# A fused convolution block: the last channel group finished bank by bank, with half snapshots and x added by VectorE

## The chip, the cores and the metric

The kernel runs on one core of a Trainium2 chip. The metric is the device time of one execution in microseconds (us). Its engines are TensorE (PE, matmuls), VectorE (DVE), ScalarE (ACT), GpSimd (POOL, used here mostly to issue DMAs) and SyncE (SP, which only issues DMAs). TensorE writes into PSUM banks; the other tiles named here lie in SBUF. DMAs move data between SBUF and HBM, whoever issues them, on the same 16 DMA engines.

## The reference

x has the shape (16, 256, 56, 56). The reference adds to x the product of a convolution and a map:

```python
xn = (x - mean) * lax.rsqrt(var + EPS)          # of the group-normed x, over batch and pixels
xn = xn * bn_gamma[None, :, None, None] + bn_beta[None, :, None, None]
t = jnp.where(xn >= 0.0, 1.0, 0.0)
t = jnp.where(xn <= 0.0, -1.0, t).astype(xn.dtype)
xc = jnp.clip(xn, -1.0, 1.0)
c_sum = jnp.sum(xc * t, axis=1, keepdims=True)
c_cnt = jnp.sum(jnp.abs(t), axis=1, keepdims=True)
y = _conv_nchw(t, conv_w, STRIDE, PAD) + conv_b[None, :, None, None]      # 3x3, 256 to 256 channels
b_sum = _conv_nchw(c_sum, ones_k, STRIDE, PAD) + beta_conv_b[0]
b_cnt = _conv_nchw(c_cnt, ones_k, STRIDE, PAD) + beta_conv_b[0]
return y * (b_sum / b_cnt)
...
x = x + _L0_conv_ref(_gn(x), ...)
```

## The kernel before

**Tiling.** An image n (0 to 15) is worked on in four groups g. A group is one half of the 256 output channels (g % 2, 128 partitions) times one half of the rows (g // 2, 28 rows, 1568 pixels for each partition). The 28 rows are 7 quads of four rows; `quads(t)` is the view [partition, quad, row of the quad, column]. The 3x3 convolution is done with a transform along the rows: for each quad six planes of transformed input (`V`) are multiplied with six planes of transformed weights (`U`), and each product plane has one row per quad, 7 x 56 = 392 elements.

**Products.** `products` (line 558) issues 24 matmuls of 128x128 weights by 385 or 392 columns: 12 (`TERMS`) into each of two PSUM banks, `acc[:, g % 2, bank]`. A group gets three such calls: `first`, `second` and `third`. They accumulate into the same two banks. After `first`, and again after `second`, ScalarE copies both banks to `sn` (`snapshot`, line 435, one ACTIVATE of 784 elements), and TensorE waits for the copy (`snap1`, `snap2`) before it goes on, since the snapshot must not contain the next planes. For image n TensorE's order (`image`, line 595) is first(g), third(g - 1), second(g) for g = 0 to 3, so that a snapshot is normally covered by another group's block. After image 15 only `third(15, 3)` is left (line 628), directly behind `second(15, 3)`.

**From products to output.** VectorE does for each group:
- `mid` (line 844): `ds` from the two snapshots (784 elements, line 849), then the rows 1 and 2 of each quad into `y` (lines 854 and 856).
- `ends` (line 860), after `third`: rows 0 and 3 of each quad from the two banks of `acc` and from `ds` (line 865, twice 392 elements).
- `finish` (line 870): y = (y + conv bias) * map, 1568 elements (line 877).
Then POOL's queue adds x by an accumulating load of x into y (line 335) and stores y (line 330), in the order: load of group s, store of group s - 1. A `mid` waits for the store of the group of the image before that used the same part of y (`y_out[g]`).

**The last group.** For (15, 3) there is no accumulating load. `finish` is done in two parts (`LAST_PARTS`, by contiguous pixels, 784 each), and `add_last` (line 880) adds x by VectorE from `xb`, which still holds image 15. SP stores each part as it comes (line 282): 128 rows of 3136 bytes. VectorE's order at the end (lines 955 to 971) is mid(15,0), ends(15,0), finish(14,3), mid(15,1), ends(15,1), finish(15,0), mid(15,2), finish(15,1), ends(15,2), finish(15,2), mid(15,3), ends(15,3), and then finish and add for each part. ScalarE's last instructions (lines 518 to 521) are the snapshots alone.

Other names: `crow`, `sum_rows`, `bm` and `map_rows` carry the map (its rows of 56 floats, 224 bytes, are written to HBM at line 246 and its sums are read back at line 217); `sum_rows` is written at line 213 in pieces of 128 bytes.

Of the kernel before, what the change touches and what calls it, by code (L numbers as in the profile page):

```python
# [8 lines left out]
ALU = mybir.AluOpType  # L9
# [29 lines left out]

LAST_PARTS = ((0, N // 2), (N // 2, N))  # L40


def conv_preact(nc, x, w_t, gamma, beta, conv_b, beta_b, consts, sum_rows, map_rows, out):
# [6 lines left out]
    with ExitStack() as ctx:  # L50
# [63 lines left out]
        y_out = [sem(f"y_out{g}") for g in range(G4)]  # L114
        last_out = [sem(f"last_out{k}") for k in range(2)]
        x_added = [sem(f"x_added{g}") for g in range(G4)]
# [68 lines left out]
        def _(sp):  # L185
# [93 lines left out]

            for k, (lo, hi) in enumerate(LAST_PARTS):  # L280
                sp.wait_ge(last_added, k + 1)
                sp.dma_start(out_v[NI - 1, 1, 1][:, 4 * lo:4 * hi], y[:, 3, 4 * lo:4 * hi]).then_inc(last_out[k], 16)
            for g in range(G4):

                sp.wait_ge(y_out[g], 16 * (NI - (g == 3)))
            for k in range(2):
                sp.wait_ge(last_out[k], 16)
# [3 lines left out]
        def _(pool):  # L291
# [39 lines left out]

            for s in range(G4 * NI - 1):
                n, g = divmod(s, G4)
                pool.wait_ge(scaled, s + 1)
                pool.dma_start(y[:, g], x_v[n, g % 2, g // 2], accum_op=ALU.add).then_inc(x_added[g], 16)  # L335
                if s:
                    store(s - 1)
            store(G4 * NI - 2)


        @block.scalar
        def _(act):
# [174 lines left out]
            channel_sums(last)  # L517
            for g in range(1, G4):
                snapshot(last, g - 1, 1)
                snapshot(last, g, 0)  # L520
            snapshot(NI - 1, 3, 1)


        @block.tensor
        def _(pe):
# [31 lines left out]

            def products(n, a, g, planes, done, by_channels=False, banks=(0, 1)):

                h, co = g // 2, g % 2  # L560
                for part in range(CT if by_channels else 1):
                    if by_channels:
                        pe.wait_ge(v_first, part + 1)
                    for bank in banks:
                        k = planes[bank]
                        for i, (ci, digits, dx) in enumerate(TERMS):
                            if by_channels and ci != part:
                                continue
                            lo, hi = max(0, 1 - dx), W - max(0, dx - 1)
                            last = nc.tensor.matmul(  # L570
                                by_row(acc[:, g % 2, bank, 0:N])[:, :, lo:hi],
                                U[:, ci, digits, k, dx, co * P:(co + 1) * P],
                                by_row(V[:, a, ci, VPLANE[k], h])[:, :, lo + dx - 1:hi + dx - 1],
                                start=(planes is FIRST and i == 0),
                                stop=(planes is THIRD and i == len(TERMS) - 1), skip_group_check=True)
                if 1 in banks:
                    last.then_inc(done, 1)

            def first(n, a, g, by_channels=False, banks=(0, 1)):

                if 0 in banks:
                    at_least(pe, y03_done, 4 * n + g - 1)
                products(n, a, g, FIRST, first_done, by_channels, banks)

            def second(n, a, g):

                pe.wait_ge(snap1, 4 * n + g + 1)
                products(n, a, g, SECOND, second_done)

# [4 lines left out]

            def image(n, a):
                for g in range(G4):
                    if g % 2 == 0:
                        pe.wait_ge(v_ready, 4 * n + 2 + g)
                    first(n, a, g)
                    if g == 0:  # L600
                        quarter_sums(n)
                    third(n - 1, 1 - a, 3) if g == 0 else third(n, a, g - 1)
                    second(n, a, g)

# [19 lines left out]
            with pe.Fori(0, (NI - 2) // 2) as i:  # L624
                image(2 * i + 1, 1)
                image(2 * i + 2, 0)
            image(NI - 1, 1)
            third(NI - 1, 1, 3)


        @block.vector
        def _(dve):
# [236 lines left out]

            def finish(n, g, part=None):  # L870

                s, b, h = 4 * n + g, g % 2, g // 2
                lo, hi = (4 * at for at in part or (0, N))
# [3 lines left out]
                nc.vector.scalar_tensor_tensor(out=y[:, g, lo:hi], in0=y[:, g, lo:hi], scalar=vec[:, 2, b:b + 1],  # L877
                                               in1=bmap[:, h, lo:hi], op0=ALU.add, op1=ALU.mult).then_inc(scaled, 1)

            def add_last(k):  # L880

                lo, hi = (4 * at for at in LAST_PARTS[k])
                dve.wait_ge(scaled, G4 * NI + k)
                nc.vector.tensor_tensor(y[:, 3, lo:hi], y[:, 3, lo:hi], own_rows(3)[:, lo:hi], ALU.add)\  # L884
                  .then_inc(last_added, 1)
# [125 lines left out]
```

## Time and profile before

| | us |
|---|---|
| median of 3 runs | 937.71 |
| lowest, highest | 937.62, 938.79 |
| profiled execution | 937.77 |
| its span, first to last instruction | 936.0 |
| TensorE busy | 782.9 |
| VectorE busy | 790.4 |
| ScalarE busy | 581.3 |
| POOL busy | 140.8 |

The span is the profiler's time from the first to the last instruction; 1.77 us of the profiled execution lie outside it. Times in rows are from the start of the span. The profile names an instruction by its line of the kernel before, its engine and its operands, `out<-in`. Until 175 us the statistics and the weights are prepared; then the images run at an even pace, and the last image's groups are done from some 880 us on.

### The profile page before, as it was taken

The page shows a single profiled execution, that of the slowest core. Times are in us where ns is not written, and L with a number is a line of the kernel's source. Part 1 is how long each engine was busy: PE and PEld are TensorE (multiplying, and loading weights), DVE is VectorE, ACT ScalarE, POOL GpSimd, SP SyncE. Part 2 cuts the span into 40 slices and gives each one's busy share as a digit, 9 for nine tenths or more (in the row PEclk, how much of TensorE's full clock was granted, in tenths as well). Part 3 has the DMA queues.
Part 4 walks back from the last instruction along what each step waited for, and adds up shares of the span by engine and source line. Part 5 has one row for each costly group of instructions (what it writes and reads, how often), then busy time and mean ns, then how long its engine had stood idle before and what let it go on. Part 6 is the DMA issues. An engine that isn't in the chain of part 4 may idle for free. (4 is left out here: it accounts for less than half of the span.)

```text
span 936.0 us, 12745 instructions
## 1 busy us (share of the span) xinstructions
PE 782.9 (84%) x4686; PEld 464.9 (50%) x4686; DVE 790.4 (84%) x1244; ACT 581.3 (62%) x469; POOL 140.8 (15%) x160
## 2 busy tenths in 40 slices
PE   2100003999999999999999999999999999999996
PEld 2100002555555555555555555555555555555553
DVE  4999998989888888888797979787878797879755
ACT  2043105968777777777777777776868686868310
POOL 0089300001111111101111111111111111101011
PEclk9755555999999999999999999999999999999998
DMA  9999972468888887888797969696969696958589
GB/s 360 429 408 377 411 323 70 142 182 259 252 249 231 243 238 220 265 213 275 192 296 174 314 161 318 163 310 165 308 171 297 174 297 185 293 157 215 131 214 268
DMA packets 43478, 232.79 MB, mean 249 GB/s; under 512 B 10560, under 2 KB 10688, under 8 KB 39360
## 3 DMA queue, kind: packets, MB, share of 16 engines
q0 software_dynamic: 18144, 101.16, 41.8%
q1 hardware_dynamic: 24544, 131.25, 38.7%
q10 hardware_dynamic: 768, 0.12, 0.1%
q8 instruction: 9, 0.15, 0.1%
q14 instruction: 13, 0.11, 0.0%
HBM read 180.73 MB, written 51.79 MB: 248 GB/s over the span
## 5 line engine op out<-in xcount | busy, mean ns | idle before, releaser
L570 PE MATMUL acc<-V,U 128*128 128x385 f16 (+1 forms) x4608 | 769.4, 331 | 11.8 <-DVE V L790 10.1
L570 PEld LDWEIGHTS acc<-V,U 128*128 128x128 f16 x4608 | 450.9, 98 | 325.8 <-issue 12.7
L442 ACT ACTIVATE sn<-acc,inv_s 128x784 f32<-128x784 f32 x128 | 116.9, 913 | 207.1 <-PE acc L570 201.2
L335 POOL DMA_DIRECT2D y<-x x63 | 53.9, 856 | 728.7 <-DVE y L877 715.2
L877 DVE SCALAR_TENSOR_TENSOR y<-y,vec,bmap 128x1568 f32<-128x1568 f32 (+1 forms) x65 | 117.7, 1810 | 0.2
L420 ACT ACTIVATE r<-xb,ab 128x1568 f32<-128x1568 f32 x64 | 106.6, 1690 | 6.0 <-ACT u L395 4.0
L395 ACT ACTIVATE u<-xb,ab 128x1624 f16<-128x1624 f32 x63 | 109.0, 1732 | 0.2
L405 ACT ACTIVATE T<-u 128x1680 f16<-128x1680 f16 x60 | 95.6, 1594 | 2.0 <-DVE D L784 2.0
L408 ACT ACTIVATE T<-T 128x1568 f16<-128x1568 f16 x58 | 87.6, 1510 | 1.8
L543 PE MATMUL csum<-mv,cst 128*128 128x32 f32 x2 | 0.6, 396 | 94.9 <-DVE mv L654 94.9
L784 DVE TENSOR_TENSOR D<-T 128x1568 f16<-128x1568 f16 x63 | 61.4, 974 | 15.1 <-ACT T L408 14.3
L849 DVE SCALAR_TENSOR_TENSOR ds<-sn 128x784 f32<-128x784 f32 x64 | 62.0, 968 | 5.9 <-ACT sn L442 5.9
L662 DVE BATCH_NORM_STATS2 st<-y 128x6 f32<-128x448 f32 x112 | 60.2, 600 | 6.6 <-DMA y<-x 6.5
L819 DVE SCALAR_TENSOR_TENSOR ssum<-r 128x1568 f32<-128x1568 f32 x32 | 57.3, 1791 | 3.5 <-ACT r L426 2.0
L826 DVE TRANSPOSE_TENSOR_REDUCE quarter<-ssum 128x49 f32<-128x1568 f32 x32 | 57.8, 1805 | 0.1
L662 DVE BATCH_NORM_STATS2 st<-xb 128x6 f32<-128x448 f32 x98 | 52.6, 598 | 6.1 <-DMA xb<-x 6.1
L330 POOL DMA_DIRECT2D out<-y x63 | 51.7, 821 | 9.9 <-DMA y<-x 9.3
L777 DVE TENSOR_SCALAR T<-T 128x784 f16<-128x784 f16 x64 | 22.5, 351 | 32.8 <-ACT T L405 32.6
L426 ACT ACTIVATE r<-r 128x1568 f32<-128x1568 f32 x32 | 48.4, 1511 | 1.0
L865 DVE SCALAR_TENSOR_TENSOR y<-acc,inv_s,ds 128x392 f32<-128x392 f32 x64 | 39.7, 620 | 9.8 <-PE acc L570 9.8
L543 PEld LDWEIGHTS csum<-mv,cst 128*128 128x128 f32 x2 | 0.5, 313 | 94.9 <-issue 94.9
L854 DVE SCALAR_TENSOR_TENSOR y<-sn,ds 128x392 f32<-128x392 f32 x64 | 36.3, 568 | 9.3 <-DMA out<-y 2.7
(99 smaller groups left out, 396.2 us busy)
## 6 DMA issues: line engine op xcount, KB each, us to landing
xb<-x SPq DMA_DIRECT2D x64, 812.0 KB, 6.4
y<-x POOLq DMA_DIRECT2D x63, 784.0 KB, 7.7
out<-y POOLq DMA_DIRECT2D x63, 784.0 KB, 9.4
y<-x SPq DMA_DIRECT2D x16, 1568.0 KB, 8.3
bmap<-map_rows SPq DMA_DIRECT2D x32, 784.0 KB, 6.1
xb<-x SPq DMA_DIRECT2D x14, 1568.0 KB, 8.7
V<-w_t SPq DMA_DIRECT2D x2, 1152.0 KB, 14.6
out<-y SPq DMA_DIRECT2D x2, 392.0 KB, 2.8
```

The lines of the kernel that those rows point to most:

```text
L395: nc.scalar.activation(u[:, g % 2, 1:1 + XR], by_row(xb[:, c, g // 2]), ACT.Sign, scale=ab[:, a, 0, c:c + 1], bias=ab[:, a, 1, c:c + 1])\
L405: nc.scalar.activation(T[:, 30:60], u[:, g % 2, h:h + HR + 2], ACT.Relu, scale=2.0).then_inc(t_ready, 1)
L408: nc.scalar.activation(T8[:, :], T[:, 30:30 + HR], ACT.Copy, scale=4.0, bias=-3.0)\
L420: nc.scalar.activation(r[:, c, 0:HPX], own_rows(g), ACT.Abs, scale=ab[:, a, 0, c:c + 1], bias=ab[:, a, 1, c:c + 1]).then_inc(abs_done, 1)
L442: nc.scalar.activation(sn[:, b, half], acc[:, b, :, 0:N], ACT.Copy, scale=inv_s[:, b:b + 1])\
L570: last = nc.tensor.matmul(by_row(acc[:, g % 2, bank, 0:N])[:, :, lo:hi], U[:, ci, digits, k, dx, co * P:(co + 1) * P], by_row(V[:, a, ci, ...
L662: ins = nc.vector.bn_stats(st[:, a, c, j], stat_buffer(a, c)[:, j * PIECE:(j + 1) * PIECE])
L784: nc.vector.tensor_tensor(d[:, 0], T[:, 32:32 + HR], T8[:, :], ALU.subtract).then_inc(cq_done, 1)
L819: nc.vector.scalar_tensor_tensor(out=ssum[:, :], in0=r[:, 0, 0:HPX], scalar=1.0, in1=r[:, 1, 0:HPX], op0=ALU.min, op1=ALU.subtract).then_i ...
L826: nc.vector.tensor_reduce(quarter[:, h, :], ssum[:, :].rearrange("p (b i) -> p b i", i=SQ), AX.X, ALU.add, apply_transpose=True).then_inc( ...
L849: nc.vector.scalar_tensor_tensor(out=ds[:, :, :], in0=sn[:, b, 0], scalar=2.0, in1=sn[:, b, 1], op0=ALU.mult, op1=ALU.subtract).then_inc(d ...
L877: nc.vector.scalar_tensor_tensor(out=y[:, g, lo:hi], in0=y[:, g, lo:hi], scalar=vec[:, 2, b:b + 1], in1=bmap[:, h, lo:hi], op0=ALU.add, op ...
```

## The change

Four things are changed, all for the last groups of image 15.

TensorE: `first(15, 3)` is issued for bank 0, then `third(15, 2)`, then `first(15, 3)` for bank 1. In each of first, second and third of (15, 3) a semaphore is raised after bank 0 as well as at the end, and the waits for snapshots are by bank.

ScalarE: each of the two snapshots of (15, 3) is taken as two halves, one a bank.

VectorE: `last_mid` forms `ds` bank by bank; `last_end(k)` forms row 0 (k = 0) or row 3 (k = 1) of each quad when that bank's third products are done; `last_finish(k)` then finishes and adds x for rows 0 to 2, and afterwards for row 3 (`LAST_ROWS`). `add_x(2)` adds x for the whole of (15, 2).

Queues: POOL no longer loads x for (15, 2) nor stores it; SP stores (15, 2) after `add_x(2)`, and then the two parts of (15, 3): per partition 7 pieces of 3 rows (672 bytes), and 7 pieces of one row (224 bytes).

```diff
-LAST_PARTS = ((0, N // 2), (N // 2, N))
+LAST_ROWS = ((0, 3), (3, 4))
...
-            for k, (lo, hi) in enumerate(LAST_PARTS):
-                sp.wait_ge(last_added, k + 1)
-                sp.dma_start(out_v[NI - 1, 1, 1][:, 4 * lo:4 * hi], y[:, 3, 4 * lo:4 * hi]).then_inc(last_out[k], 16)
+            sp.wait_ge(last_added, 1)
+            sp.dma_start(out_v[NI - 1, 0, 1], y[:, 2]).then_inc(last_out[2], 16)
+            for k, (lo, hi) in enumerate(LAST_ROWS):
+                sp.wait_ge(last_added, k + 2)
+                sp.dma_start(quads(out_v[NI - 1, 1, 1])[:, :, lo:hi].rearrange("p q i w -> p q (i w)"),
+                             quads(y[:, 3])[:, :, lo:hi].rearrange("p q i w -> p q (i w)")).then_inc(last_out[k], 16)
...
-            for s in range(G4 * NI - 1):
+            for s in range(G4 * NI - 2):
...
-            store(G4 * NI - 2)
+            store(G4 * NI - 3)
...
-            for g in range(1, G4):
+            for g in range(1, G4 - 1):
                 snapshot(last, g - 1, 1)
                 snapshot(last, g, 0)
-            snapshot(NI - 1, 3, 1)
+            snapshot(last, 2, 1)
+            act.wait_ge(mid_done, G4 * NI - 2)
+            for half, done, part_done, snap, part_snap in ((0, first_done, first_half, snap1, snap1_half),
+                                                           (1, second_done, second_half, snap2, snap2_half)):
+                for bank in range(2):
+                    if bank:
+                        act.wait_ge(done, G4 * NI)
+                    else:
+                        act.wait_ge(part_done, 1)
+                    nc.scalar.activation(sn[:, 1, half, bank], acc[:, 1, bank, 0:N], ACT.Copy, scale=inv_s[:, 1:2])\
+                      .then_inc(snap if bank else part_snap, 1)
...
+                        if half is not None and bank == 0:
+                            last.then_inc(half, 1)
+                            if planes is SECOND:
+                                pe.wait_ge(snap1, G4 * NI)
+                            if planes is THIRD:
+                                pe.wait_ge(snap2, G4 * NI)
                 if 1 in banks:
                     last.then_inc(done, 1)
...
-                    first(n, a, g)
+                    last = final and g == 3
+                    if last:
+                        first(n, a, g, banks=(0,), half=first_half)
+                    else:
+                        first(n, a, g)
                     if g == 0:
                         quarter_sums(n)
                     third(n - 1, 1 - a, 3) if g == 0 else third(n, a, g - 1)
-                    second(n, a, g)
+                    if last:
+                        first(n, a, g, banks=(1,))
+                    second(n, a, g, second_half if last else None)
...
-            image(NI - 1, 1)
-            third(NI - 1, 1, 3)
+            image(NI - 1, 1, final=True)
+            pe.wait_ge(snap2_half, 1)
+            products(NI - 1, 1, 3, THIRD, third_done, half=third_half)
...
+            def add_x(g):
+
+                dve.wait_ge(scaled, G4 * NI - 3 + g)
+                nc.vector.tensor_tensor(y[:, g], y[:, g], own_rows(g), ALU.add).then_inc(last_added, 1)
+
+            def last_mid():
+
+                last = G4 * NI
+                for bank in range(2):
+                    if bank:
+                        dve.wait_ge(snap2, last)
+                    else:
+                        dve.wait_ge(snap2_half, 1)
+                        dve.wait_ge(y03_done, last - 1)
+                    ins = nc.vector.scalar_tensor_tensor(out=ds[:, bank], in0=sn[:, 1, 0, bank], scalar=2.0,
+                                                         in1=sn[:, 1, 1, bank], op0=ALU.mult, op1=ALU.subtract)
+                ins.then_inc(ds_done, 1)
+                dve.wait_ge(y_out[3], 16 * (NI - 1))
+                dve.wait_ge(ds_done, last)
+                yq = quads(y[:, 3])
+                nc.vector.scalar_tensor_tensor(out=yq[:, :, 1], in0=by_row(sn[:, 1, 1, 1]), scalar=2.0,
+                                               in1=by_row(ds[:, 0]), op0=ALU.mult, op1=ALU.add)
+                nc.vector.scalar_tensor_tensor(out=yq[:, :, 2], in0=by_row(ds[:, 1]), scalar=4.0,
+                                               in1=by_row(sn[:, 1, 1, 0]), op0=ALU.mult, op1=ALU.add)\
+                  .then_inc(mid_done, 1)
+                dve.wait_ge(mid_done, last)
+
+            def last_end(k):
+
+                if k:
+                    dve.wait_ge(third_done, G4 * NI)
+                else:
+                    dve.wait_ge(third_half, 1)
+                nc.vector.scalar_tensor_tensor(
+                    out=quads(y[:, 3])[:, :, 3 * k], in0=by_row(acc[:, 1, k, 0:N]), scalar=(inv_s, inv_8)[k][:, 1:2],
+                    in1=by_row(ds[:, 1 - k]), op0=ALU.mult, op1=ALU.add).then_inc(y03_done, 1)
+                dve.wait_ge(y03_done, G4 * NI + k)
+
+            def last_finish(k):
+
+                lo, hi = LAST_ROWS[k]
+                part = lambda t: quads(t)[:, :, lo:hi].rearrange("p q i w -> p q (i w)")
+                dve.wait_ge(bmap_in[1], 16 * NI)
+                nc.vector.scalar_tensor_tensor(out=part(y[:, 3]), in0=part(y[:, 3]), scalar=vec[:, 2, 1:2],
+                                               in1=part(bmap[:, 1]), op0=ALU.add, op1=ALU.mult).then_inc(scaled, 1)
                 dve.wait_ge(scaled, G4 * NI + k)
-                nc.vector.tensor_tensor(y[:, 3, lo:hi], y[:, 3, lo:hi], own_rows(3)[:, lo:hi], ALU.add)\
+                nc.vector.tensor_tensor(part(y[:, 3]), part(y[:, 3]), part(own_rows(3)), ALU.add)\
                   .then_inc(last_added, 1)
...
-            mid(NI - 1, 3)
-            ends(NI - 1, 3)
+            add_x(2)
+            last_mid()
             for k in range(2):
-                finish(NI - 1, 3, LAST_PARTS[k])
-                add_last(k)
+                last_end(k)
+                last_finish(k)
```

## Rows read from the trace of the kernel before

**Rows 1.** The page's head and part 1: busy us, share of span, instructions.

```profile
span 936.0 us, 12745 instructions
PE 782.9 (84%) x4686; PEld 464.9 (50%) x4686; DVE 790.4 (84%) x1244; ACT 581.3 (62%) x469; POOL 140.8 (15%) x160
```

**Rows 2.** Chain that ended last, its last pieces: start, us, what.

```profile
931.08 1.04 DVE y L877
...
932.14 0.98 DVE y L884
```

**Rows 3.** Timeline from 910 us: start, us, engine, line, out<-in, count [idle before].

```profile
910.52 0.86 POOL L330 DMA_DIRECT2D out<-y  x1
...
913.74 1.85 DVE L877 SCALAR_TENSOR_TENSOR y<-y,vec,bmap 128x1568 f32<-128x1568 f32 x1
914.73 0.91 ACT L442 ACTIVATE sn<-acc,inv_s 128x784 f32<-128x784 f32 x1 [3.07 <-PE acc L570]
...
918.72 0.63 DVE L865 SCALAR_TENSOR_TENSOR y<-acc,inv_s,ds 128x392 f32<-128x392 f32 x1 [3.13 <-PE acc L570]
...
922.70 0.91 ACT L442 ACTIVATE sn<-acc,inv_s 128x784 f32<-128x784 f32 x1 [7.06 <-PE acc L570]
923.42 0.56 POOL L330 DMA_DIRECT2D out<-y  x1 [0.46 <-DMA y<-x]
923.65 0.97 DVE L849 SCALAR_TENSOR_TENSOR ds<-sn 128x784 f32<-128x784 f32 x1 [1.83 <-ACT sn L442]
...
923.67 4.16 PE L570 MATMUL acc<-V,U 128*128 128x392 f16 x24 [1.01 <-ACT sn L442]
924.73 0.57 DVE L854 SCALAR_TENSOR_TENSOR y<-sn,ds 128x392 f32<-128x392 f32 x1
925.22 0.56 DVE L856 SCALAR_TENSOR_TENSOR y<-ds,sn 128x392 f32<-128x392 f32 x1
927.87 0.63 DVE L865 SCALAR_TENSOR_TENSOR y<-acc,inv_s,ds 128x392 f32<-128x392 f32 x1 [2.10 <-PE acc L570]
928.41 0.62 DVE L865 SCALAR_TENSOR_TENSOR y<-acc,inv,ds 128x392 f32<-128x392 f32 x1
929.12 1.03 DVE L877 SCALAR_TENSOR_TENSOR y<-y,vec,bmap 128x784 f32<-128x784 f32 x1
...
930.19 0.97 DVE L884 TENSOR_TENSOR y<-y,xb 128x784 f32<-128x784 f32 x1
...
931.19 2.29 SPq L282 DMA_DIRECT2D out<-y  x2
```

**Rows 4.** DMA view of 933.9 to 935.1: busy tenths in 30 ns slices; SP's queue: packets, MB, share.

```profile
DMA  0009829927597759775977595779777997753000
...
q1 hardware_dynamic: 146, 0.40, 84.9%
```

**Rows 5.** Groups of instructions, shapes apart: ACT's pass over 1568 elements, busy us, mean ns.

```profile
L420 ACT ACTIVATE r<-xb,ab 128x1568 f32<-128x1568 f32 x64 | 106.6, 1690 | 6.0 <-ACT u L395 4.0 <-DVE ssum L819 0.5
```

**Rows 6.** Line 330, the one store issued between 910 and 911 us.

```profile
DMA to landing us min/median/max: 8.3/8.3/8.3
```

**Rows 7.** Busy time by stretch, last column GB/s: with an accumulating load, then without.

```profile
925.00:927.00 2.00, 2.00 (x14) 1.17 (x12) 0.78 (x2) 0.00 (x0) 0.00 (x0) 1.00 0.87 166
...
931.00:933.00 2.00, 0.00 (x0) 0.00 (x0) 1.97 (x3) 0.00 (x0) 0.00 (x0) 0.50 0.99 403
```

**Rows 8.** Waits of SP's queue over the span: us in total, times, longest.

```profile
SPq L217 <- DMA sum_rows<-cs: 79.5, 16, 6.2
```

**Rows 9.** DMA view, 887.0 to 887.5 (`crow` read), then 889.9 to 890.5 (`bm` written).

```profile
DMA  0000000000000014634644589699877696532210
...
q1 hardware_dynamic: 175, 0.04, 37.9%
...
DMA  0000000000000000004554535321000000000000
...
q1 hardware_dynamic: 70, 0.01, 10.3%
```

More of the change, by code:

```diff
@@ L114, in conv_preact @@
         y_out = [sem(f"y_out{g}") for g in range(G4)]
-        last_out = [sem(f"last_out{k}") for k in range(2)]
+        last_out = [sem(f"last_out{k}") for k in range(3)]
+        first_half, second_half, third_half = sem("first_half"), sem("second_half"), sem("third_half")
+        snap1_half, snap2_half = sem("snap1_half"), sem("snap2_half")
         x_added = [sem(f"x_added{g}") for g in range(G4)]
@@ L278, in _ @@
             image(NI - 1)
-            for k, (lo, hi) in enumerate(LAST_PARTS):
-                sp.wait_ge(last_added, k + 1)
-                sp.dma_start(out_v[NI - 1, 1, 1][:, 4 * lo:4 * hi], y[:, 3, 4 * lo:4 * hi]).then_inc(last_out[k], 16)
+            sp.wait_ge(last_added, 1)
[4 more added lines that the diff above has]
+                             quads(y[:, 3])[:, :, lo:hi].rearrange("p q i w -> p q (i w)")).then_inc(last_out[k], 16)
             for g in range(G4):
-                sp.wait_ge(y_out[g], 16 * (NI - (g == 3)))
-            for k in range(2):
+                sp.wait_ge(y_out[g], 16 * (NI - (g > 1)))
+            for k in range(3):
                 sp.wait_ge(last_out[k], 16)
@@ L556, in quarter_sums, with products @@
                                  cst[:, C_FOLD:C_FOLD + SQ], start=True, stop=True).then_inc(cs_done, 1)
-            def products(n, a, g, planes, done, by_channels=False, banks=(0, 1)):
+            def products(n, a, g, planes, done, by_channels=False, banks=(0, 1), half=None):
                 h, co = g // 2, g % 2
@@ L575, in products, with first, second @@
                                 stop=(planes is THIRD and i == len(TERMS) - 1), skip_group_check=True)
+                        if half is not None and bank == 0:
[4 more added lines that the diff above has]
+                                pe.wait_ge(snap2, G4 * NI)
                 if 1 in banks:
                     last.then_inc(done, 1)
-            def first(n, a, g, by_channels=False, banks=(0, 1)):
+            def first(n, a, g, by_channels=False, banks=(0, 1), half=None):
                 if 0 in banks:
                     at_least(pe, y03_done, 4 * n + g - 1)
[L583 to L588, printed above, removed]
+                products(n, a, g, FIRST, first_done, by_channels, banks, half)
+            def second(n, a, g, half=None):
+                if half is None:
+                    pe.wait_ge(snap1, 4 * n + g + 1)
+                else:
+                    pe.wait_ge(snap1_half, 1)
+                products(n, a, g, SECOND, second_done, half=half)
             def third(n, a, g):
@@ L593, in third, with image @@
                 products(n, a, g, THIRD, third_done)
-            def image(n, a):
+            def image(n, a, final=False):
                 for g in range(G4):
@@ L868, in ends, with finish @@
                 ins.then_inc(y03_done, 1)
-            def finish(n, g, part=None):
+            def finish(n, g):
                 s, b, h = 4 * n + g, g % 2, g // 2
-                lo, hi = (4 * at for at in part or (0, N))
                 dve.wait_ge(mid_done, s + 1)
@@ L876, in finish @@
                 dve.wait_ge(bmap_in[h], 16 * n + 16)
[L877 to L882, printed above, removed]
+                nc.vector.scalar_tensor_tensor(out=y[:, g], in0=y[:, g], scalar=vec[:, 2, b:b + 1],
+                                               in1=bmap[:, h], op0=ALU.add, op1=ALU.mult).then_inc(scaled, 1)
@@ new lines, in last_end @@
+            def last_end(k):
+                if k:
+                    dve.wait_ge(third_done, G4 * NI)
+                else:
+                    dve.wait_ge(third_half, 1)
[9 more added lines that the diff above has]
+                                               in1=part(bmap[:, 1]), op0=ALU.add, op1=ALU.mult).then_inc(scaled, 1)
```

## The prediction

> **What bounds the kernel now.** I read three views in this order: the page's first part, the chain that ended last, and the timeline of the last 25 us. The page shows TensorE busy for 84% of the span [rows 1]; the reader should take from it only that the middle is a full pipeline which this change doesn't touch. Everything edited belongs to image 15, groups 2 and 3, so the question is what ends after about 910 us. The chain ends on VectorE: the second half of `finish` and `add_last` [rows 2]. The timeline [rows 3] shows what stands before it. TensorE's blocks of 24 matmuls follow each other at 3.99 us: `first(15,3)` ends 0.04 us before ACT's snapshot at 914.73, `third(15,2)` 0.04 before VectorE's `ends` at 918.72, `second(15,3)` 0.04 before the snapshot at 922.70. (The 0.04 is the step from TensorE's end, 923.67 + 4.16 = 927.83, to `ends` at 927.87.) So `second(15,3)` ends at 922.66, TensorE then stands 1.01 us for the full snapshot, runs `third(15,3)` to 927.83, and only there VectorE's serial tail begins: two `ends` instructions, finish, add, finish, add, to 932.14 + 0.98 = 933.12 [rows 2, 3]. The last store is then issued at about 933.14, its packets run from 933.99 to 935.00 [rows 4], and the span ends at 936.00, 1.00 after the last packet. The profiled execution took 937.77 us, 1.77 outside the span; the median of the runs shown is 937.71, so the sum below, made against 937.77, can be 0.06 high.
>
> **TensorE's new order.** `first(15,3)` is split by banks and `third(15,2)` put between. Nothing is added to the work, so the total stays at four blocks of 3.99 from 910.70: first bank 0 to 912.69, `third(15,2)` to 916.68, first bank 1 to 918.68, second bank 0 to 920.67, bank 1 to 922.66. `third(15,2)` starts 2 us earlier and needs the snapshot taken at 910.70 + 0.04, done 0.91 later (911.65): 1.04 us of slack. The half snapshots: ACT takes 0.913 for 784 elements [rows 3] and 1.690 for 1568 [rows 5], 0.99 ns an element, so 0.53 for 392. Each is done 1.4 us before the bank that waits for it (bank 0 of second: its snapshot is over at 919.3 at the latest; third bank 0: 921.3 against 922.66; third bank 1: 923.3 against 924.66). The 1.01 us stall goes, and third runs 922.66 to 924.66 and to 926.65. The cost is three more boundaries with a semaphore ahead of second's end. A block has 8 x 392 + 16 x 385 = 9296 columns, 3.87 us at the full level of 2.4 GHz, and takes 3.99, so a boundary costs from 0 to 0.12 us (not below 0: no matmul is dropped). I take 0.03 each, 0.10 in all, up to 0.35.
>
> **VectorE ahead of the tail.** With `third(15,2)` done at 916.68, `ends(15,2)` starts at 916.72, after `finish(15,1)` is over at 915.59 [rows 3]; it and `finish(15,2)` (1.85, by the same row) end at 919.8. `add_x(2)` is new: an add of 1568 elements; the 784-element add took 0.97 [rows 3] and another 784 elements cost 0.81 (1.85 - 1.03, finish whole less finish half), so 1.78, to 921.6. Behind it on VectorE waits ds of bank 0, ready at 921.3: 0.57, over at 922.2, before bank 1's snapshot at 923.3. So it is hidden by 1.1 us of idle time; without that cover it would cost its 1.78. `last_mid` also waits for the store of group (14,3), issued at 910.52 [rows 3] and landed 8.3 us later [rows 6], some four microseconds early.
>
> **VectorE's tail.** Gaps by rows of before: 0.04 after ACT; 0.11 from ds to the instruction that needs it (924.62 to 924.73); 0.49 from start to start of the two mid instructions; 0.09 behind a mid or an `ends` whose result is waited for; 0.04 from finish to add; an unrelated next one starts 0.09 before the end of an add (930.19 + 0.97 against 931.08) [rows 2, 3]. With the 0.10: second ends at 922.76, ACT 922.80 to 923.33, ds bank 1 (0.57) 923.37 to 923.94, mid 924.05 and 924.54 to 925.10. Then `ends` bank 0 925.19 to 925.81 (third bank 0 is done by 924.8, so VectorE, not TensorE, decides from here), finish of three rows in four, 1176 elements, 1.03 + 0.40 = 1.43, 925.90 to 927.33; its add 0.97 + 0.40 = 1.37, 927.37 to 928.74; `ends` bank 1 928.65 to 929.27; finish of 392 elements 0.63, 929.36 to 929.99; add 0.57, 930.03 to 930.60. Against 933.12 that is 2.52 us earlier: 1.0 from the stall, the rest because mid and bank 0's end and finish run under third.
>
> **The queues.** The accumulating load and the store of (15,2) leave POOL, and SP stores (15,2) itself at 921.6. SP's following waits (for the two last parts) stand behind an issue of 0.34 us only. What is in flight from 921.7: the end of the accumulate of (15,1), the stores of (15,0) and (15,1) (the latter issued at 923.42 [rows 3], behind that accumulate as now) and SP's: 3 x 128 x 1568 x 4 B, 2.4 MB. Plain stores moved 403 GB/s, a stretch with an accumulate 166 [rows 7]; so 6.0 us and about 1 more for what remains of the accumulate: empty at 928.7 to 929. The first last part is issued at 928.76 with its first packet 0.85 later (933.14 to 933.99), at 929.6: clear by 0.6 us. It must be, for a small store behind this traffic landed badly: SP waited 79.5 / 16 = 5.0 us for each 98-row store of `sum_rows` [rows 8].
>
> **The scattered last stores.** They were 128 packets of 3136 B each. Now they follow rows: 7 pieces for each of 128 partitions, 896 packets of 672 B and 896 of 224 B, 56 each for an engine and one for the semaphore. Nearest rows: the 3136 B packets took 0.849 x 16 x 1.2 / 146 = 0.112 each with the semaphores' (about 0.125 without) [rows 4]; the 224 B reads of `crow` 0.379 x 16 x 0.5 / 175 = 0.017 of busy time; their busy stretch is some 25 slices of 12.5 ns for 13 packets an engine, 0.024 in elapsed time (the `bm` store of 56 rows shows 70 packets, 14 over, so I read one completion each on 14 engines; `crow` has 168 rows, 12 an engine and the completion); the 224 B writes of `bm` 0.103 x 16 x 0.6 / 70 = 0.014 of busy time, and elapsed ten slices of 15 ns for 5, 0.030 [rows 9]. By the line between 0.017 and 0.125, 672 B takes 0.034: 1.9 us, to 931.5. The last part, issued at 930.62, has its first packet at 931.5 too; 57 packets take 1.0 (busy time of the reads), 1.4 (their elapsed time) or 1.7 (elapsed of the writes). I take 1.4, since five packets are mostly ramp, and keep both ends. Last packet at 932.9, span's end 1.00 later, at 933.9: 2.1 us earlier. This gives back 0.4 of the 2.5. 937.77 - 2.1 = 935.7.
>
> The rule of the Trainium skill that speaks against this part is in "DMA: Bandwidth & Descriptors", Specifications: transfers under 512 B fall below line rate because the engine does a read-modify-write. The `bm` writes of 224 B don't show it in busy time, 0.014 against 0.017 for reads [rows 9]. By the rule, taken as twice the 1.0, the last part would take 1.9 to 2.0 and the time be 936.2 to 936.3; the same direction is rival 1, priced from rows.
>
> **The rivals.** (1) Short rows cost more when written in bulk. For it: the elapsed 0.030 of the only 224 B writes, 0.013 over the 0.017; against it: their busy time of 0.014. With 0.030 for the last part and 0.034 + 0.013 for the 672 B rows: 929.6 + 2.7 + 1.7 = 934.0, end 935.0, time 936.8. (2) The queues aren't empty at 929.6, since the stores move at 300 GB/s beside the accumulate instead of 403: they clear about 1 us late, 936.7. For it: stretches with an accumulate are slow; against: 0.6 us of margin and none issued after 915.88. (3) All the small terms fall well: boundaries free (0.1), last part at busy pace (0.4): 935.2. (4) Slower: the same last stores, at a pace like that of the `sum_rows` rows. The time is 929.6 + 114 t + 1.0 + 1.77 for a pace of t an engine and packet: equal to before at t = 0.047, slower by 0.2% from t = 0.064, and 941.5 at 0.08. For it: `sum_rows` with 7 packets an engine took 5 us; against: that one stood behind POOL's traffic, and the `crow` rows kept 0.024. (5) The change does not do what it says: a half's snapshot comes late or `add_x` holds VectorE, so that ds of bank 1 starts no earlier than 924.4; then half the gain stays, 936.8.
>
> **How the numbers follow.** Forecast 935.7 (its own range 935.2 to 936.2) 0.52; rival 3 0.13; rival 1 0.18; rival 2 0.07; rival 5 0.04; rival 4 0.06. The range leaves out rival 4 and the outer ends: 934.9 to 937.4. A measurement of this kernel tells about 0.2% from no change, 1.88 us, so faster by more means below 935.83: 0.6 of the forecast's 0.52 and rival 3's 0.13, with a little of the others, 0.47. Slower 0.06, and within 0.2% 0.47.
>
> **What would show it.** Right: no idle time of TensorE between `second(15,3)` and third, and its last matmul at 926.7 to 926.9; VectorE without a gap over 0.15 us from ds bank 1 (923.3 to 923.6) to its last add, which ends at 930.4 to 930.9; `add_x(2)` over before 922; the packets of SP's last two stores from 929.6 to 932.5 to 933.6. Wrong: last add early and packets past 934 (rival 1 or 4); other queues' packets after 929.6 (rival 2); a wait for ACT or a late start of ds bank 1 (rival 5).

## The result and the profile after

| | before | after |
|---|---|---|
| median of 13 runs each, us | 938.22 | 935.95 |
| lowest, us | 937.28 | 934.99 |
| profiled execution, us | 937.77 | 936.13 |
| its span, us | 935.97 | 934.32 |

The ratio is 0.9970, with a 95% interval of 0.9959 to 0.9980: faster by 0.3%, and the interval ends just at 0.2%. The page gives a span to a tenth of a microsecond; the traces keep nanoseconds, and those are used here: 935.97 and 934.32. The two differ by only 1.65 us, less than the medians (2.27). The reason can be seen as soon as both timelines are laid side by side: in the profiled execution of after, image 15 is 0.80 us late before anything that was changed is reached. So all that follows is counted from one mark which no kernel here moves, the start of ScalarE's snapshot after `first(15,2)`: at 902.77 before and 903.57 after. From there to the end of the span it is 33.20 us before and 30.75 after, 2.45 less; two later profiles of the same changed kernel gave 30.75 again. (The expectations below were written with the rounded spans, 33.23 and 30.73, and a tail of 3.11 and 2.88 where the traces have 3.13 and 2.85.) The mark in the timeline of before:

```profile
902.77 0.91 ACT L442 ACTIVATE sn<-acc,inv_s 128x784 f32<-128x784 f32 x1 [3.07 <-PE acc L570]
```

The timeline of after (start, us, engine, line, operation, out<-in, [idle before]) at the instructions that answer to [rows 3]. L585 is the matmul, L535 the half snapshots, L896 the first `ends` instruction of (15,2), L913 `add_x`, L924 to L956 the last group:

```profile
902.70 24.75 PE L585 MATMUL acc<-V,U 128*128 128x385 f16 x148
...
903.57 0.91 ACT L447 ACTIVATE sn<-acc,inv_s 128x784 f32<-128x784 f32 x1 [3.07 <-PE acc L585]
...
917.52 0.63 DVE L896 SCALAR_TENSOR_TENSOR y<-acc,inv_s,ds 128x392 f32<-128x392 f32 x1 [1.15 <-PE acc L585]
...
920.65 1.79 DVE L913 TENSOR_TENSOR y<-y,xb 128x1568 f32<-128x1568 f32 x1
...
923.50 0.59 ACT L535 ACTIVATE sn<-acc,inv_s 128x392 f32<-128x392 f32 x1 [1.41 <-PE acc L585]
...
924.12 0.57 DVE L924 SCALAR_TENSOR_TENSOR ds<-sn 128x392 f32<-128x392 f32 x1 [1.19 <-ACT sn L535]
924.79 0.57 DVE L930 SCALAR_TENSOR_TENSOR y<-sn,ds 128x392 f32<-128x392 f32 x1
925.27 0.56 DVE L932 SCALAR_TENSOR_TENSOR y<-ds,sn 128x392 f32<-128x392 f32 x1
925.87 0.63 DVE L943 SCALAR_TENSOR_TENSOR y<-acc,inv_s,ds 128x392 f32<-128x392 f32 x1
926.53 1.44 DVE L953 SCALAR_TENSOR_TENSOR y<-y,vec,bmap 128x1176 f32<-128x1176 f32 x1
928.01 1.38 DVE L956 TENSOR_TENSOR y<-y,xb 128x1176 f32<-128x1176 f32 x1
929.31 0.62 DVE L943 SCALAR_TENSOR_TENSOR y<-acc,inv,ds 128x392 f32<-128x392 f32 x1
929.42 2.18 SPq L286 DMA_DIRECT2D out<-y  x2
929.96 0.63 DVE L953 SCALAR_TENSOR_TENSOR y<-y,vec,bmap 128x392 f32<-128x392 f32 x1
930.62 0.57 DVE L956 TENSOR_TENSOR y<-y,xb 128x392 f32<-128x392 f32 x1
```

Three things are to be seen. TensorE is one piece to 927.45; the idle 1.01 us of [rows 3] is gone. From the mark its last matmul ends 1.18 us earlier: the 1.01, and 0.17 because `third(15,3)` takes the 3.99 us of the other blocks and not the 4.16 that it took after the wait [rows 3]. From 924.12 VectorE has one instruction behind the other, none with an idle time of note, to 930.62 + 0.57 = 931.19. And from there to the span's end it is 3.13 us, where it was 2.85 (933.12 to 935.97). So VectorE's last add ends 2.73 us earlier from the mark (27.63 for 30.35), and what follows it is 0.28 longer.

The DMA view of after, 926 to 935 in slices of 0.225 us, against [rows 4] and [rows 7]:

```profile
DMA  9999999999983000000499999999999600000000
GB/s 446 418 418 418 418 418 446 418 446 418 418 335 140 0 0 0 0 0 0 155 329 317 323 320 317 317 248 286 278 271 268 142 1 0 0 0 0 0 0 0
```

This view counts a packet where it starts. The last packet of the groups before starts at 928.92 and ends at 929.16; the engines then stand idle until 930.36, when the first of the two last stores begins. The 672-byte pieces move at about 320 GB/s, the 224-byte ones at about 270, and the last packet ends at 933.23.

### The profile page after: what moved, and what is told of

It reads as the page before. It is cut to its first block, busy times and chain, and to the rows that moved or that the text cites. A ratio compares the mean times of both kernels' runs of the same rounds, so it can differ in the third digit from the quotient of the medians.

```text
span 934.3 us, 12748 instructions
## 1 busy us (share of the span) xinstructions
PE 781.9 (84%) x4686; PEld 464.5 (50%) x4686; DVE 792.2 (85%) x1246; ACT 582.1 (62%) x471; POOL 139.7 (15%) x158
## 4 chain that ended last, share of the span: by engine, by line
PE 77%; DVE 17%; DMA 3%; issue 2%; ACT 1%; SPq 0%; DVEq 0%; ACTq 0%
PE acc L585 77%; DVE st L693 11%; DMA xb<-x 2%; DVE st L704 1%; DMA sum_rows<-cs 1%; DVE y L907 1%; DVE D L815 0%; ACT r L425 0%; DVE y L896 0%; DVE ds L880 0%; DVE V L825 0%; DVE y L953 0%; DVE D L813 0%; DVE V L826 0%; DVE quarter L857 0%
## 5 line engine op out<-in xcount | busy, mean ns | idle before, releaser
L585 PE MATMUL acc<-V,U 128*128 128x385 f16 (+1 forms) x4608 | 769.6, 330 | 10.8 <-DVE V L821 10.1
L585 PEld LDWEIGHTS acc<-V,U 128*128 128x128 f16 x4608 | 451.3, 98 | 324.6 <-issue 13.1
L907 DVE SCALAR_TENSOR_TENSOR y<-y,vec,bmap 128x1568 f32<-128x1568 f32 x63 | 115.6, 1835 | 0.1
L808 DVE TENSOR_SCALAR T<-T 128x784 f16<-128x784 f16 x64 | 22.5, 351 | 32.8 <-ACT T L410 32.6
L896 DVE SCALAR_TENSOR_TENSOR y<-acc,inv_s,ds 128x392 f32<-128x392 f32 x63 | 39.1, 620 | 5.8 <-PE acc L585 5.8
```

Source lines behind the costliest of these rows:

```text
L585: last = nc.tensor.matmul(by_row(acc[:, g % 2, bank, 0:N])[:, :, lo:hi], U[:, ci, digits, k, dx, co * P:(co + 1) * P], by_row(V[:, a, ci, ...
L907: nc.vector.scalar_tensor_tensor(out=y[:, g], in0=y[:, g], scalar=vec[:, 2, b:b + 1], in1=bmap[:, h], op0=ALU.add, op1=ALU.mult).then_inc( ...
```

## The experiments

All nine edits were judged from the mark, since the median of a few runs can't tell parts of a microsecond of this kernel. "Tail" is the time from the end of VectorE's last add to the end of the span. Ratios are to the kernel before on the same chip.

**Only TensorE's and ScalarE's part**

```diff
# of the changed kernel, back as before (SP's last two stores too):
-            add_x(2)
-            last_mid()
-            for k in range(2):
-                last_end(k)
-                last_finish(k)
+            mid(NI - 1, 3)
+            ends(NI - 1, 3)
+            for k in range(2):
+                finish(NI - 1, 3, LAST_PARTS[k])
+                add_last(k)
...
+            for s in range(G4 * NI - 1):       # POOL loads and stores (15,2) again
```

> Only TensorE's and ScalarE's part of the change: first(15,3) by banks with third(15,2) between, half snapshots. VectorE, POOL and SP as before. All cases are counted from one mark that the change doesn't touch, the start of ScalarE's snapshot after first(15,2), to the end of the span: 33.23 us before, 30.73 after. Theory (the stall of 1.01 us stood on the path, and all VectorE work behind third moves with it): TensorE has no idle time between second and third of group 3, ends starts 1.2 us earlier from the mark, VectorE's tail keeps its 5.25 us, mark to end 32.0. Rival (VectorE's own work in front of ends, or POOL's store of group 2, is next in line at once): ends starts 0.4 us earlier at most, mark to end 32.8.

Measured: mark (904.50) to end 32.65; ratio 0.9997 (0.9982 to 1.0012). The timeline:

```profile
925.05 0.98 DVE L877 SCALAR_TENSOR_TENSOR ds<-sn 128x784 f32<-128x784 f32 x1 [3.50 <-ACT sn L532]
...
928.42 0.63 DVE L893 SCALAR_TENSOR_TENSOR y<-acc,inv_s,ds 128x392 f32<-128x392 f32 x1 [1.24 <-PE acc L582]
...
931.04 0.55 POOL L332 DMA_DIRECT2D out<-y  x1 [5.45 <-DMA y<-x]
...
931.74 2.29 SPq L284 DMA_DIRECT2D out<-y  x2
932.69 0.97 DVE L912 TENSOR_TENSOR y<-y,xb 128x784 f32<-128x784 f32 x1
```

The theory's VectorE part holds: `ends` starts 23.92 after the mark instead of 25.10, and the last add ends at 933.66, 29.17 after it, 1.19 earlier than before. But the end of the span is only 0.56 earlier, nearer to the rival's 32.8 than to the theory's 32.0: the tail is 3.48 us. The rival was right in naming POOL's store of group 2, though not in a late `ends`: that store is issued at 931.04 and SP's last stores from 931.74, so that both are in the queues together for longer than before (there 929.70 and 931.19). The gain of the stall is real and half of it is lost; that the DMA queues take it is shown by the run after the next.

**Only group (15,2)**

```diff
# of the kernel before:
-            for s in range(G4 * NI - 1):
+            for s in range(G4 * NI - 2):
...
+            sp.wait_ge(x2_added, 1)
+            sp.dma_start(out_v[NI - 1, 0, 1], y[:, 2]).then_inc(last_out[2], 16)
...
+            add_x(2)
             mid(NI - 1, 3)
```

> Only the part on group (15,2): VectorE adds its x and SP stores it, POOL's accumulating load and store of it are gone; group 3 as before. Theory: nothing, mark to end 33.1 to 33.3 (from 33.23), since the add of 1.79 us lies in VectorE's idle time ahead of the last ds and the last store of before was not behind POOL's packets. Rival (POOL's traffic held up the last stores): the first of the two last stores lands in 2.3 us instead of 3.2 and the span ends 0.5 us earlier, 32.7. Rival (the added instruction delays the last mid): 33.6 or more.

Measured: mark (903.46) to end 33.26, VectorE's last add 30.35 after the mark, as before; ratio 0.9997 (0.9988 to 1.0007). By itself this part is worth nothing (the end is even 0.06 later): the theory.

**Banks and group 2, with the old tail of group 3**

```diff
# the two edits above together; VectorE's end is
+            add_x(2)
             mid(NI - 1, 3)
             ends(NI - 1, 3)
```

> The banks-only kernel with group (15,2) moved as in the change (VectorE adds x, SP stores), while group 3 keeps the old tail: one ds of 784 elements, both ends, then finish and add by contiguous halves. Theory (the two parts need each other: banks give 1.2 us only if POOL's accumulate and store are out of the way): VectorE's last add ends 29.15 us after the mark, as with banks only, and the span 2.9 later, at 32.05, where banks only had 32.6 and group 2 only 33.24. What is left to the change's 30.72 is then the bank-wise tail of group 3. Rival (the late last stores of the banks-only run had another cause): tail of 3.4, 32.6.

Measured: mark (903.69) to end 32.08, last add 29.17, tail 2.91; ratio 0.9997 (0.9983 to 1.0010).

```profile
930.94 2.29 SPq L287 DMA_DIRECT2D out<-y  x2
931.89 0.97 DVE L920 TENSOR_TENSOR y<-y,xb 128x784 f32<-128x784 f32 x1
```

The last add is where it was with the banks alone, and the tail is that of the run with group 2 alone (2.91), so it was POOL's traffic that had stretched it to 3.48. (This interval can't see the 1.12 us, 0.12%; the timeline can.)

**The change without its group (15,2)**

```diff
# of the changed kernel:
-            for s in range(G4 * NI - 2):
+            for s in range(G4 * NI - 1):
...
-            add_x(2)
             last_mid()
```

> The changed kernel, but group (15,2) goes through POOL's queue again (accumulating load, then store), without VectorE's add of it. Theory (from the banks-only run, where VectorE's last add ended 29.16 us after the mark and the last stores then stood behind POOL's store of group 2): POOL's store is still issued about 26.5 us after the mark, when the accumulating load has landed, the first of SP's last stores meets it, and the span ends 32.0 to 32.8 after the mark instead of 30.73, with VectorE's last add still at 27.6. Rival (the DMA engines have room for both): 30.7 to 31.0. Rival (the short pieces take turns with POOL's packets of 6272 bytes and crawl): 34 or more.

Measured: mark (903.81) to end 33.31; ratio 1.0000 (0.9988 to 1.0013). The direction was foreseen, the size (32.0 to 32.8) was not: the whole gain is gone, with VectorE as early as in the changed kernel. Its timeline, and its DMA queues from 930 us to the end (queue: packets, MB, share of the engines; then SP's two stores: KB, us from issue to landing):

```profile
929.67 2.19 SPq L284 DMA_DIRECT2D out<-y  x2
930.21 0.55 POOL L333 DMA_DIRECT2D out<-y  x1 [5.17 <-DMA y<-x]
930.22 0.63 DVE L951 SCALAR_TENSOR_TENSOR y<-y,vec,bmap 128x392 f32<-128x392 f32 x1
930.88 0.57 DVE L954 TENSOR_TENSOR y<-y,xb 128x392 f32<-128x392 f32 x1
```

```profile
q0 software_dynamic: 229, 1.24, 43.5%
q1 hardware_dynamic: 1824, 0.80, 39.8%
...
out<-y SPq DMA_DIRECT2D x1, 588.0 KB, 6.1
out<-y SPq DMA_DIRECT2D x1, 196.0 KB, 5.2
```

The last add ends at 931.44, 27.63 after the mark, and 5.68 us follow it. POOL's queue still moves 1.24 MB after 930.0; SP's two stores land 6.1 and 5.2 us after issue instead of 3.5 and 2.5. The engines are busy for 83% of these 7.1 us, and the last 1.1 us of them come behind the last packet; each of SP's packets takes as long as in the changed kernel (0.034 and 0.016 us by the trace). So this is a queue of bytes in front of the last ones, not a crawl.

**`third(15,2)` not put between the banks**

```diff
# of the changed kernel:
-                        first(n, a, g, banks=(0,), half=first_half)
+                        first(n, a, g, half=first_half)
...
-                    if last:
-                        first(n, a, g, banks=(1,))
```

> The changed kernel, but first(15,3) runs whole before third(15,2); half snapshots and bank-wise second and third stay. Theory (the order matters only by letting VectorE finish group 2 earlier): TensorE has no stall either way, third(15,2) ends 2 us later, the x add of group 2 ends about 1.9 us later, the ds of bank 1 starts 0.8 us late, mark to end 31.5 instead of 30.73. Rival (it serves to cover the snapshots): a stall of 0.5 us on TensorE comes back. Rival (the order is worth nothing): 30.7.

Measured: mark (904.58) to end 31.46, close to the theory; ratio 0.9984 (0.9973 to 0.9995).

```profile
900.72 27.74 PE L585 MATMUL acc<-V,U 128*128 128x385 f16 x166
...
923.66 1.79 DVE L911 TENSOR_TENSOR y<-y,xb 128x1568 f32<-128x1568 f32 x1
...
925.37 1.03 DVE L922 SCALAR_TENSOR_TENSOR ds<-sn 128x392 f32<-128x392 f32 x2
```

TensorE is one piece without the interleaving too (to 928.46, 23.88 after the mark, as in the changed kernel), so the half snapshots, with their waits by bank, remove the stall without it. What the new order brings is 0.71 us, and on VectorE: the x add of group 2 ends 2 us earlier, so both halves of ds no longer wait behind it.

**The last stores contiguous** (from x, so that group (15,3) of the output is x alone)

```diff
-                sp.dma_start(quads(out_v[NI - 1, 1, 1])[:, :, lo:hi].rearrange("p q i w -> p q (i w)"),
-                             quads(y[:, 3])[:, :, lo:hi].rearrange("p q i w -> p q (i w)")).then_inc(last_out[k], 16)
+                sp.dma_start(out_v[NI - 1, 1, 1][:, N * lo:N * hi], own_rows(3)[:, N * lo:N * hi]).then_inc(last_out[k], 16)
```

> The changed kernel with its last two stores made contiguous: 4704 and 1568 bytes for each partition, taken from x instead of y (so the output of group (15,3) is x alone; the waits and all computation stay). Theory (the pieces of 672 and 224 bytes cost 0.4 us): last add's end to the span's end 2.7 us instead of 3.11, mark to end 30.3. Rival (short pieces cost nothing in bulk): 3.1 and 30.7. Rival (they cost double and more, a write below 512 bytes being read first): under 2.5 and under 30.1.

Measured: mark (904.05) to end 30.09, tail 2.47; ratio 0.9968 (0.9952 to 0.9984). Against the 3.13 of the changed kernel, the short pieces cost 0.66 us, more than the theory's 0.4. By the expectation's numbers this would be the double price of a short write; the next experiment shows it isn't.

**All rows of group (15,3) in pieces of 224 bytes**

```diff
+                for i in range(lo, hi):
+                    sp.dma_start(quads(out_v[NI - 1, 1, 1])[:, :, i], quads(y[:, 3])[:, :, i]).then_inc(last_out[k], 16)
```

> The changed kernel with the first of the two last stores cut into three stores of single rows, so that all four rows go in pieces of 224 bytes (3584 instead of 1792 packets for the same bytes). It measures what a 224-byte packet costs in bulk. Theory (0.0155 us of a DMA engine for each, as the last store's packets show): 112 more packets an engine, where 56 of 672 bytes (0.031 each) are replaced by 168: 2.6 us instead of 1.7, span's end 0.9 us later, mark to end 31.6. Rival (a store under 512 bytes costs double): 168 at 0.031 or more, 5.2 us, mark to end 34 or more. Rival (SP's issue of 0.38 us for each of the four stores sets the pace): 31.5 as well, but with idle DMA engines between the stores.

Measured, in one execution: mark (903.70) to end 32.07, tail 4.44. The DMA view from 930.5 to 934.5:

```profile
DMA  7999899999888999898888989988899999999994
...
q1 hardware_dynamic: 3646, 0.80, 100.9%
```

One short packet took 1.009 x 16 x 4.0 / 3646 = 0.0177 us, in a full queue of 3646, at 201 GB/s. The reads of [rows 9] had 0.017. The end at 32.07 is far from the 34 of the double price, and the engines have no idle stretch between the stores, so SP's issue does not set the pace either. The excess of 0.47 us over the theory's 31.6 is about what 0.0177 in place of 0.0155 makes in 228 packets an engine (0.50).

In the changed kernel itself the two sizes can be read apart, 672 bytes from 930.5 to 931.5 and 224 bytes from 932.5 to 932.9:

```profile
DMA packets 479, 0.32 MB, mean 322 GB/s; under 512 B 0, under 2 KB 479, under 8 KB 479
q1 hardware_dynamic: 479, 0.32, 98.7%
...
DMA packets 483, 0.11 MB, mean 270 GB/s; under 512 B 483, under 2 KB 483, under 8 KB 483
q1 hardware_dynamic: 483, 0.11, 117.2%
```

A packet of 672 bytes takes 0.987 x 16 x 1.0 / 479 = 0.033 us, one of 224 bytes 1.172 x 16 x 0.4 / 483 = 0.0155. A share above 100% means that packets of one engine overlap: one starts every 16 x 0.4 / 483 = 0.013 us. Why the same pieces go at 270 GB/s here and at 201 when 3646 of them stand in the queue was not isolated.

**POOL takes a part of the tail** (a version made to be faster)

```diff
+            nc.gpsimd.tensor_tensor(e0, by_row(ds[:, 1]), quads(bmap[:, 1])[:, :, 0], ALU.mult)
...
+            nc.gpsimd.tensor_tensor(e0, e0, quads(own_rows(3))[:, :, 0], ALU.add)
...
+            nc.gpsimd.tensor_tensor(rows12(y[:, 3]), rows12(y[:, 3]), rows12(own_rows(3)), ALU.add)
```

> A version made to be faster. x plus bias times map of group (15,3) is formed early in an idle stretch of VectorE (1.84 us); ds of bank 0 times map plus that, for row 3, in the idle 1.2 us before ds of bank 1; the same for row 0 and the x add of rows 1 and 2 on POOL (about 0.92 and 1.84 us, from 2.35 ns an element in its 768-element instructions, beside VectorE). After third only one product with the map for each bank and one add of 784 elements are left, then one contiguous store of the whole group by SP. Theory (VectorE's serial work after the last snapshot is the bound): VectorE's last add ends 25.6 us after the mark instead of 27.6, the store needs 3.9 us from there to the span's end (2.88 for half of it, and 1.0 for the other half's packets), mark to end 29.5 instead of 30.73. Rival (POOL beside a busy VectorE is slower than alone, and its two products for row 0 and its add are then last): 30.7 or more.

Measured: mark (904.23) to end 31.42, last add 27.54 after the mark; ratio 0.9986 (0.9974 to 0.9997). The rival's time. Its timeline:

```profile
925.53 1.37 POOL L348 TENSOR_TENSOR ssum<-ds,bmap 128x392 f32<-128x392 f32 x1
925.94 1.39 DVE L955 SCALAR_TENSOR_TENSOR y<-ds,sn 128x392 f32<-128x392 f32 x1
926.98 1.22 POOL L350 TENSOR_TENSOR ssum<-ssum,xb 128x392 f32<-128x392 f32 x1
927.36 1.67 DVE L960 TENSOR_TENSOR y<-y,bmap 128x784 f32<-128x784 f32 x1
...
929.11 1.84 POOL L352 TENSOR_TENSOR y<-y,xb 128x784 f32<-128x784 f32 x1 [0.91 <-DVE y L960]
929.49 0.61 DVE L967 SCALAR_TENSOR_TENSOR y<-acc,inv,bmap 128x392 f32<-128x392 f32 x1
930.13 1.64 DVE L973 TENSOR_TENSOR y<-y,ssum 128x784 f32<-128x784 f32 x1
```

But POOL's instructions are not last, as the rival had it: they made VectorE's longer, an instruction of 0.56 took 1.39, two of 0.97 took 1.67 and 1.64. POOL's two short ones became longer too, 1.37 and 1.22 for the expected 0.92; its long add kept the expected 1.84. The two engines took turns: L955 ends 0.43 us after POOL's L348, POOL's L350 0.87 after L955, L960 0.83 after L350, and L973 0.82 after POOL's add, each a little less than the instruction needs alone (0.56, the expected 0.92, 0.97 and 0.97). L967, with one input in PSUM, kept its 0.61 beside POOL's add. The Trainium skill ("SBUF — State Buffer", Who interferes with whom) has the rule: a VectorE instruction with two SBUF inputs contends with a GpSimd instruction that reads SBUF, over a pair of ports that one of them locks, and one with at most one SBUF input (outside the modes that use both of VectorE's port pairs) does not contend. The trace agrees with both halves. The tail, with one contiguous store of the whole group, was 3.87, near the expected 3.9.

**The rows finished one after the other, without POOL** (a version made to be faster)

```diff
+                nc.vector.tensor_tensor(by_row(e[:, 1]), by_row(ds[:, 0]), bq[:, :, 3], ALU.mult).then_inc(e_step, 1)
...
+                nc.vector.tensor_tensor(by_row(e[:, 1]), by_row(e[:, 1]), xq[:, :, 3], ALU.add).then_inc(e_step, 1)
...
+                times_map_and_x(1, 3, 1)
...
+                nc.vector.tensor_tensor(yq[:, :, 3], yq[:, :, 3], by_row(e[:, 1]), ALU.add).then_inc(last_added, 1)
...
+                times_map_and_x(0, 1, 2)
```

> A version made to be faster, without POOL. x plus bias times map of group (15,3) is formed early in an idle stretch of VectorE, and ds of bank 0 times map plus that, for row 3, in the idle 1.2 us before ds of bank 1. Then rows 1 and 2 are finished and stored, then row 3 (one product and one add after third), then row 0 (three instructions), each stored by SP in pieces of 448, 224 and 224 bytes. Theory (VectorE's serial work bounds the last add; the last store should be small): last add ends 27.2 us after the mark instead of 27.6, last store's packets 28.05 to 29.1, mark to end 30.15 instead of 30.72, that is 0.06% faster than the changed kernel. Rival (more short pieces keep the DMA engines busy past VectorE's end): 30.7 or more. Rival (the added 1.84 us instruction delays group 2's mid and all behind it): last add later than 27.6.

Measured: mark (904.12) to end 30.12; ratio to before 0.9963 (0.9947 to 0.9979), where the changed kernel beside it had 0.9978 (0.9966 to 0.9990).

```profile
928.44 3.25 SPq L289 DMA_DIRECT2D out<-y  x3
928.98 0.57 DVE L970 TENSOR_TENSOR y<-y,ssum 128x392 f32<-128x392 f32 x1
929.47 0.62 DVE L971 SCALAR_TENSOR_TENSOR y<-acc,inv_s,ds 128x392 f32<-128x392 f32 x1
930.12 0.57 DVE L958 TENSOR_TENSOR y<-y,bmap 128x392 f32<-128x392 f32 x1
930.72 0.57 DVE L961 TENSOR_TENSOR y<-y,xb 128x392 f32<-128x392 f32 x1
```

The last add ends 27.16 after the mark (931.29), as worked out, 0.47 before that of the changed kernel, and the tail is 2.96, 0.17 shorter. By the mark it is the fastest of the kernels that compute the whole output, 0.63 us ahead of the changed kernel. The two intervals overlap, so the runs alone don't show it.

**The changed kernel again.**

> The changed kernel once more on the same chip, as the measure for the others: 0.997 of the time before, mark to end 30.7, last add's end to the span's end 3.1.

> The changed kernel once more, as the measure for the version above on the same chip: 0.997 to 0.9975 of the time before, mark to end 30.7.

Measured: marks 903.29 and 903.58, mark to end 30.75 and last add 27.63 in both; ratios 0.9975 (0.9963 to 0.9987) and 0.9978 (0.9966 to 0.9990). The expectation's numbers hold.

## Why the prediction was right

The forecast was 935.7 us in a range of 934.9 to 937.4; the median came out at 935.95. The mechanism is the one that was forecast: from the mark, the prediction had VectorE's last add 2.52 us earlier and gave 0.4 back for the stores; it was 2.73 and 0.28, so 2.45 for the 2.1 forecast. That the time itself was met within 0.25 is partly luck: the sum started from 937.77, while the 13 runs of before have their median at 938.22, and the larger gain made up for most of that. Step by step:

- **The stall.** Right: 1.01 us of TensorE's idle time gone. The three boundaries, taken at 0.10, cost nothing (`second(15,3)` ends 19.89 after the mark, as 922.66 does before). The experiments add which edit does it: the half snapshots, not the interleaving.
- **The half snapshot** was a term a little too small: 0.59 us for 392 elements and not 0.53. The slope between 784 and 1568 elements came from another kind of ScalarE instruction [rows 5].
- **VectorE ahead of the tail.** Right: `add_x` 1.79 (1.78 worked out). When group 2 came 2 us later, 0.71 reached the end, since the idle time ahead of the last ds took the rest; the full 1.78, named for no cover at all, was not tried.
- **VectorE's tail.** Every duration was met within 0.01 us; the gaps were too large. Behind the second mid instruction and behind an `ends` the prediction took 0.09 from the place in [rows 3] where three waits follow each other; in the new order these gaps are 0.03 to 0.04. Why they are shorter was not isolated. The gaps (some 0.2 in all) and the boundaries (0.10), less the snapshot's 0.06, are the 0.21.
- **The queues.** The rival of a queue still busy when the last stores come was given 0.07 and did not happen: the last packet ahead of them ended at 929.16, 1.2 us before their first one. The prediction saw the edit on group 2 as a point to be cleared; it did not see that it carries the whole change. It looked only at what is in flight with the edit, and never asked what bank-wise work would give without it. The answer, 33.31 against 30.75, is the largest number of this study.
- **The short pieces.** The forecast has 3.3 us from the last add to the end, 3.13 were measured, and that near only because errors of opposite sign met. Too much: the last part's packets were given 1.4 us, from the elapsed time of 13 packets, and took 0.95 (932.28 to 933.23). Too little: their first one was put 0.9 after the last add and came 1.09 after it, behind the end of the first part (930.36 to 932.47, 2.1 us for 1.9). With contiguous stores it came 0.86 after. And the end of the span was put 1.00 behind the last packet, read in [rows 4] from where that packet starts; it ends at 935.12, 0.85 before the end of the span. In the changed kernel it is 1.09, and why it is longer behind short packets was not isolated. That the tail as a whole grew by only 0.28 comes from the last part being 200 KB instead of 401: contiguous stores with the same split needed 2.47 where before had 2.85, and the short pieces put 0.66 on that.
- **The slower rival** needed 0.064 us for each of 114 packets in a row; they took 0.025 (930.36 to 933.23). The double price, as which the prediction took the read-modify-write of the Trainium skill, was not seen either: 0.0155 and 0.0177 for 224 bytes, 0.033 for 672, 0.125 for 3136 [rows 4] lie near one line.

From the mark, in 33.20 us: TensorE's and ScalarE's banks take off 0.56 by themselves and 1.12 together with group 2; group 2 by itself -0.06; the bank-wise tail of VectorE, with its short pieces, the other 1.33 (32.08 to 30.75). They don't add up part by part, because the end waits for VectorE's last add and for what stands in the DMA queues ahead of the last store.

What stays open: how much of the difference between the medians (2.27) and the profiles (2.45 from the mark) is only scatter. The runs of one kernel are 4 us apart here and over, and the mark itself moved by 1.8 us between profiles (902.77 to 904.58) with no change ahead of it.

## What to carry to other kernels

Before a tail is shortened, ask what stands in the DMA queues at the moment at which the tail will then end: a step that frees them can be worth nothing alone and everything together, so single edits tried one at a time would have thrown away this one. To judge tenths of a microsecond, count in the trace from an instruction that no version moves; three profiles of the changed kernel agreed to 0.002 us in it, where single runs scattered by whole ones. The ends have to be read as finely as the starts: a span rounded to a tenth had put up to 0.05 us on every such number. And before work is lent to another engine, ask whether the two will take turns, as VectorE and POOL did here when both read two operands from SBUF.

## What the runs showed of the hardware

- SP's stores to HBM: a packet of 224 bytes takes 0.0155 us (last part of the changed kernel, 270 GB/s) or 0.0177 (3646 of them in the queue, 201 GB/s), one of 672 bytes 0.033 (322 GB/s), one of 3136 bytes 0.125 [rows 4]: about 0.008 a packet and the rest by size, with no step below 512 bytes.
- VectorE and POOL, both reading two operands from SBUF, take turns by whole instructions (VectorE's 0.56 became 1.39 and 0.97 became 1.64 to 1.67, POOL's expected 0.92 became 1.22 and 1.37). I had expected only POOL to be slowed.
- ScalarE's half snapshot costs 0.59 where the whole one costs 0.91: splitting in two adds 0.27 us of its time, here idle.
- TensorE's block of 24 matmuls took 4.16 us after an idle 1.01 us [rows 3] and 3.99 in the row of blocks.
